# Chain ends and layer outputs of a CIN kernel: from a PSUM bank to SBUF, and a ring of six banks

## The chip, the cores and the metric

One NeuronCore of a Trainium2 chip runs the kernel. The metric is the device time of one launch in microseconds. The engines are TensorE (PE), VectorE (DVE), ScalarE (ACT) and GpSimd (POOL); SyncE (SP) issues DMAs. On-chip data lies in SBUF or in PSUM, where the matmuls of this kernel write. The kernel uses eight PSUM tensors of 512 fp32 columns, called banks below.

## The reference, cut to what matters

512 samples, 48 embedding fields of 32 elements each, gathered from 48 tables. Three "CIN" layers of 128 outputs follow, and a small top network:

```python
def _cin_layer(xi, x0, W, b):                     # xi (n, Fi, 32), x0 (n, 48, 32)
    Wr = W.reshape(Fi, 48, 128)
    out = jnp.einsum('nie,nje,ijo->noe', xi, x0, Wr) + b[None, :, None]
    return jax.nn.relu(out)
xs = [x0]
for W, b in ((W1, b1), (W2, b2), (W3, b3)):
    xs.append(_cin_layer(xs[-1], x0, W, b))
z = jnp.concatenate(xs, axis=1).sum(axis=-1)      # (512, 48 + 3*128)
h = relu([z, dense_ctx] @ W_top1 + b_top1); h = relu(h @ W_top2 + b_top2); y = h @ W_top3
```

## The kernel before

**Tiles.** A tile is 128 samples at one embedding position, so there are 4 x 32 = 128 tiles, and each goes through all three layers. Layer 1 is done through squares of pair sums and is short. For layers 2 and 3 (in the code `layer` 0 and 1) PE computes, for each of 48 fields j, y_j = x W_j of 128x128: twelve "items" a layer, each of four fields, which fill one PSUM bank `y` of 512 columns with three matmuls (hi by whi, hi by wlo, lo by whi; L474). Then out = b + sum over j of x0[:, j] * y_j has to be formed, by two routes. Items marked D in `TAKES` go to DVE, which runs for each field one `scalar_tensor_tensor` acc = y * x0_j + acc (L786; L780 and L782 are the first two of a layer). Two accumulator chains alternate, and the last instruction of each chain writes not `acc` but `chain_end` (two per layer). Items marked A go to ACT, which writes the products y * x0_j to `work` in SBUF (L572); POOL adds them up: a DMA with accumulation (L327) folds two banks of products onto two others, tensor_tensor instructions (L338, L342, L350, L352, L354, L357) sum the rest down to `psum` (an SBUF tile in spite of its name).

**Merging.** DVE's `merge` joins both: msum = chain_end[0] + psum (L795), then outp = chain_end[1] + msum (L800), where `outp` of layers 2 and 3 lies on top of chain_end[0]. From `outp` ACT forms the relu with its row sum (L609, layers 1 and 2), and the high half `hi` (L616); DVE forms the low half `lo` = outp * sc - hi (L832, layers 1 and 2) and adds relu(outp) to the pooled sums (`over_e`, L839, all three layers). SP transposes hi and lo by DMA for PE. `outp` of layer 1 lies in the bank misc[0].

**Order.** All engines run the same software pipeline of `step(v)`: in step v, PE does the twelve items of layer 2 for tile v+1 (n = 0 to 11), the twelve of layer 3 for tile v (n = 12 to 23), with layer 1 of tile v+2 and the pair sums of tile v+3 between them. The order on each engine is written out by hand. DVE's items are n = 1, 3, 5, 7, 9, 11 and 12, 14, 16, 18, 20, 22, 23. In one DVE step the merge instructions stand behind these FMAs: `lo` of layer 2 at n = 5, k = 0, `over_e` of layer 2 at n = 5, k = 1; the two merges of layer 3 at n = 9, k = 0 and 2 (between them `lo` of layer 1, then its `over_e`); `over_e` of layer 3 at n = 11, k = 0; the two merges of layer 2 at n = 20, k = 1 and 3. POOL's order in a step is: last sums of layer 3 (L350 to L357), L327 for layer 2, the scaling of x0 every other step (L368, L373), one gather DMA, L338, L342 and the last sums of layer 2, L327 for layer 3, the low half of the squares (L362, nine times 128 columns), a second gather, L342 of layer 3. The gathers of the next 32 tiles' embeddings run in 24 of the 32 steps of each of the first three blocks of samples, and four steps more copy them out (L304, `spread`); the last block has none.

**Banks.** PSUM holds `RING` = 5 banks `ybank`, two `misc` banks (layer 1 and the pair sums) and the bank `ends`, which holds the four chain ends of layers 2 and 3 and with them their `outp`. PE's item n of a step goes to ybank[n % RING]; `bank_free` makes it wait until DVE or ACT is done with the item that had the bank before (`bank_done`). With 24 items a step and RING = 5 the ring starts anew in every step: items 0 to 3 take the banks of items 20 to 23 of the step before, item 4 that of item 19, the others that of the item five back. At the very end the pooled sums are transposed through ybank[0] to [2] and `ends`.

Of the kernel before, what the change touches and what calls it, by code (L numbers as in the profile page):

```python
# [33 lines left out]
P = 128  # L34
# [11 lines left out]
Z = KT * P  # L46
Q = 4
BANKS = F // Q
RING = 5
HID1, HID2 = 512, 256  # L50


# [15 lines left out]
PAIRS_AT = (12, 14, 17)  # L68
LAST_USER = [max(m for m in range(BANKS) if (BANKS + m) % RING == r) for r in range(RING)]
SCALE = 4  # L70
# [8 lines left out]
def build(nc, ids, tables, ctx_in, select, pairs_of, w_pair, w_pair_t, w2, w3, b_cin, wt1, bt1, wt2, bt2, wt3, out):  # L79
    f32, f16, i32, u32 = mybir.dt.float32, mybir.dt.float16, mybir.dt.int32, mybir.dt.uint32  # L80
    ALU, ACT, AX = mybir.AluOpType, mybir.ActivationFunctionType, mybir.AxisListType

    with ExitStack() as stack:
        def sb(name, shape, dt=f32):
            return stack.enter_context(nc.sbuf_tensor(name, shape, dt))

        def ps(name, shape, dt=f32):
            return stack.enter_context(nc.psum_tensor(name, shape, dt))

        def sem(name):  # L90
            return stack.enter_context(nc.semaphore(name))

        def wait(eng, s, value):

            if not (isinstance(value, int) and value <= 0):
                eng.wait_ge(s, value)  # L96
# [30 lines left out]
        eye32 = sb("eye32", [P, P])  # L127
# [20 lines left out]
        pooled = sb("pooled", [P, NB + 1, 3, P])  # L148
        low = sb("low", [P, NB, F + CTX])
        hT = sb("hT", [P, 4, B])  # L150
# [12 lines left out]

        ybank = [ps(f"y{n}", [P, Q * P]) for n in range(RING)]
        misc = [ps(f"m{n}", [P, Q * P]) for n in range(2)]
        ends = ps("ends", [P, Q * P])

        chain_end = [[ends[:, (2 * l + c) * P:(2 * l + c + 1) * P] for c in range(CHAINS)] for l in range(2)]

# [37 lines left out]
        s_tt, s_tts, s_low, s_h1p, s_h1, s_h2p, s_h2, s_yp, s_ys, s_out = (  # L207
            sem(n) for n in ("hT_in_psum", "hT_saved", "low_ready", "h1_in_psum", "h1_ready", "h2_in_psum",
                             "h2_ready", "y_in_psum", "y_saved", "y_stored"))

        def bank_done(eng, layer, tile, n):

            if n in A_BANKS[layer]:
                wait(eng, s_prod[layer], tile * PRODS[layer] + Q * (A_BANKS[layer].index(n) + 1))
            else:
                wait(eng, s_fma[layer], tile * FMAS[layer] + Q * (D_BANKS[layer].index(n) + 1))
# [12 lines left out]
        def active(tile):  # L229

            return not isinstance(tile, int) or 0 <= tile < TILES
# [186 lines left out]
        def _(pe):  # L418
# [4 lines left out]
            for k in range(KT):  # L423
                ins = nc.tensor.matmul(misc[0][0:F, 0:P], member[:, k, :], w1s[:, k, :], start=k == 0, stop=k == KT - 1)
# [3 lines left out]
            for g in range(2):  # L428
                ins = nc.tensor.transpose(misc[0][0:1, g * P:(g + 1) * P], wmax[:, 8 + g:9 + g], eye32[:])
# [38 lines left out]
            def y_item(layer, t, m, parity):  # L468
                if m == 0:
                    wait(pe, s_xt[layer], (t + 1) * 32)  # L470
                dst = ybank[(layer * BANKS + m) % RING]
                cols = slice(m * Q * P, (m + 1) * Q * P)
# [4 lines left out]
            def bank_free(v, n):  # L477


                for back, first in ((0, n - RING), (1, 2 * BANKS - 1)):  # L480
                    for i in range(first, -1, -1):
                        layer, tile = i // BANKS, v + 1 - i // BANKS - back
                        if i % RING == n % RING and active(tile):
                            return bank_done(pe, layer, tile, i % BANKS)
# [17 lines left out]
            last = TILES - 1  # L502
            pe.wait_ge(s_top, 8 * 16)
            for l in (0, 1):
                pe.wait_ge(s_pool[l], TILES + 1)
                bank_done(pe, 1, last, LAST_USER[l])
                for b in range(NB):
                    ins = nc.tensor.transpose(ybank[l][:, b * P:(b + 1) * P], pooled[:, b, l, :], eye32[:])
# [3 lines left out]
            for b in range(NB):  # L512
                ins = nc.tensor.transpose(ybank[2][0:F + CTX, b * P:(b + 1) * P], low[:, b, :], eye32[:])
# [6 lines left out]
            for i, c in enumerate(CHUNKS):  # L520
                if i == 2:
                    pe.wait_ge(s_pool[2], TILES + 1)
                    for b in range(NB):
                        ins = nc.tensor.transpose(ends[:, b * P:(b + 1) * P], pooled[:, b, 2, :], eye32[:])
                    ins.then_inc(s_tt, 1)
                pe.wait_ge(s_tts, i + 1)
                k = F + CTX if c == 0 else P
                for m in range(HID1 // P):
                    ins = nc.tensor.matmul(h1bank[m][:], wt1_sb[0:k, c, m * P:(m + 1) * P], hT[0:k, c, :],
                                           start=i == 0, stop=c == 3)  # L530
                    if c == 3:
                        ins.then_inc(s_h1p, 1)
            for c in range(HID1 // P):
                pe.wait_ge(s_h1, c + 1)
                for m in range(HID2 // P):
                    ins = nc.tensor.matmul(ybank[m][:], wt2_sb[:, c, m * P:(m + 1) * P], h1[:, c, :],
                                           start=c == 0, stop=c == HID1 // P - 1)
                    if c == HID1 // P - 1:
                        ins.then_inc(s_h2p, 1)
            for c in range(HID2 // P):  # L540
                pe.wait_ge(s_h2, c + 1)
                ins = nc.tensor.matmul(ybank[2][0:1, :], wt3_sb[:, c:c + 1], h2[:, c, :],
                                       start=c == 0, stop=c == HID2 // P - 1)
# [4 lines left out]
        def _(act):  # L548

            act.wait_ge(s_wchain, 16)  # L550
            for l in range(2):
                nc.scalar.activation(whi[l][:], raw[l], ACT.Copy, scale=winv[:, 0:1]).then_inc(s_split, 1)
                for n in range(BANKS):
                    i = l * BANKS + n
                    if i >= RING:
                        act.wait_ge(s_setup, W1_SETUP + i - RING + 1)
# [94 lines left out]
            for i, c in enumerate(CHUNKS):  # L651
                k = F + CTX if c == 0 else P
                act.wait_ge(s_tt, i + 1)
                nc.scalar.activation(hT[0:k, c, :], (ybank[2], ybank[0], ybank[1], ends)[c][0:k, :], ACT.Copy).then_inc(s_tts, 1)
            act.wait_ge(s_top, 8 * 16)
            h1bank = [misc[0], misc[1], ybank[3], ybank[4]]
            for m in range(HID1 // P):
# [297 lines left out]
```

## Time and profile before

| | us |
|---|---|
| median of 3 runs (2443.72 to 2446.77) | 2445.55 |
| the profiled execution | 2444.75 |
| its span in the trace | 2442.9 |
| work before the first item of layer 2 (loads, scales, weights split) | 85.2 |
| last item of layer 3 starts | 2415.0 |

| engine | busy us | share of the span |
|---|---|---|
| PE | 2325.3 | 95% |
| DVE | 2278.7 | 93% |
| ACT | 2117.9 | 87% |
| POOL | 1953.0 | 80% |

Busy time is the union of the instructions' spans. An instruction's duration in the trace is longer than the distance at which the next one follows, so a duration is not what an instruction costs: cost is the distance from one start to the next on the same engine. Three numbers with slashes are the least, median and greatest duration of a group in ns.

### The profile page before, as it was taken

What the parts mean: (1) busy time and instruction counts of PE and PEld (TensorE: products, weight loads), DVE (VectorE), ACT (ScalarE), POOL (GpSimd) and SP (SyncE); (2) the same over time, 40 slices, a digit from 0 to 9 for tenths busy, and PEclk for the clock granted to TensorE, in tenths of its full rate; (3) what the DMA queues carried; (4) which work ended last, traced back from release to release, by engine and by line L of the source; (5) the groups of instructions that cost most, each with busy time, mean ns of one, the idle gap of its engine ahead of it and who ended that gap; (6) DMA issues with size and microseconds to landing.
All of it is one profiled execution on the core that took longest, in us unless ns stands there. A gap on an engine that the chain in (4) does not pass through costs nothing.

```text
span 2442.9 us, 68954 instructions
## 1 busy us (share of the span) xinstructions
PE 2325.3 (95%) x14174; PEld 1178.2 (48%) x14174; DVE 2278.7 (93%) x9404; ACT 2117.9 (87%) x7910; POOL 1953.0 (80%) x2134
## 2 busy tenths in 40 slices
PE   1699999999999999999999999999999999999998
PEld 0354454454554554444455445445445555555543
DVE  6499999999999999999999999999999999999995
ACT  4589889889898898888898888988889989999984
POOL 7488888887778888888778888888777777777773
PEclk6799999999999999999999999999999999999999
DMA  5133333333333333333333333333333333333331
GB/s 170 30 68 72 69 66 70 70 69 64 69 70 66 69 72 70 63 72 70 61 70 70 70 64 71 72 65 68 70 62 70 67 69 70 69 70 69 69 64 35
DMA packets 150318, 168.63 MB, mean 69 GB/s; under 512 B 111956, under 2 KB 115671, under 8 KB 150264
## 3 DMA queue, kind: packets, MB, share of 16 engines
q0 software_dynamic: 43008, 137.39, 30.4%
q1 hardware_dynamic: 107256, 30.73, 5.7%
q14 instruction: 46, 0.38, 0.1%
q8 instruction: 8, 0.13, 0.0%
HBM read 12.82 MB, written 0.00 MB: 5 GB/s over the span
## 4 chain that ended last, share of the span: by engine, by line
PE 42%; POOL 16%; issue 13%; ACT 10%; DVE 9%; DMA 8%; DVEq 1%; ACTq 0%; POOLq 0%; SPq 0%
PE y L474 35%; DMA work<-work 8%; ACT work L572 6%; DVE acc L786 5%; PE m L464 5%; POOL part L350 4%; POOL emb L295 3%; POOL part L354 2%; POOL part L352 2%; ACT work L602 1%; POOL psum L357 1%; POOL rest L342 1%; PE m L446 1%; POOL work L327 1%; DVEq L96 1%
## 5 line engine op out<-in xcount | busy, mean ns | idle before, releaser
L474 PE MATMUL y<-whi,xT 128*128 128x512 f16 x6144 | 2006.9, 379 | 38.8 <-DVE acc L786 24.3
L572 ACT ACTIVATE work<-y,xc 128x128 f32<-128x128 f32 x5632 | 1604.9, 417 | 182.7 <-PE y L474 172.1
L786 DVE SCALAR_TENSOR_TENSOR acc<-y,xc,acc 128x128 f32<-128x128 f32 x5632 | 1654.5, 343 | 32.8 <-PE y L474 24.1
L474 PE MATMUL y<-wlo,xT 128*128 128x512 f16 x3072 | 1164.8, 379 | 0.0
L474 PEld LDWEIGHTS y<-whi,xT 128*128 128x128 f16 x6144 | 599.0, 97 | 692.3 <-issue 77.9
L474 PEld LDWEIGHTS y<-wlo,xT 128*128 128x128 f16 x3072 | 300.8, 98 | 227.8 <-issue 0.6
L350 POOL TENSOR_TENSOR part<-work 128x512 f32<-128x512 f32 x256 | 325.4, 1271 | 90.8 <-DMA work<-work 66.5
L362 POOL TENSOR_TENSOR zl<-work,zh 128x1152 f16<-128x1152 f32 x128 | 345.0, 2695 | 8.1 <-ACT work L602 8.1
L327 POOL DMA_DIRECT2D work<-work x256 | 229.2, 895 | 128.4 <-ACT work L572 127.0
L295 POOL DMA_INDIRECT emb<-tbl,ids_sb x192 | 202.5, 1055 | 45.0 <-issue 43.9
L600 ACT ACTIVATE zh<-m 128x512 f16<-128x512 f32 (+1 forms) x384 | 212.2, 553 | 3.1 <-PE m L446 3.1
L602 ACT ACTIVATE work<-m 128x512 f32<-128x512 f32 (+1 forms) x384 | 214.9, 560 | 0.0
L338 POOL TENSOR_TENSOR part<-work 128x512 f32<-128x512 f32 x128 | 164.5, 1285 | 54.2 <-ACT work L572 54.2
L352 POOL TENSOR_TENSOR part<-part 128x256 f32<-128x256 f32 x256 | 186.0, 727 | 20.1
L354 POOL TENSOR_TENSOR part<-part,rest 128x256 f32<-128x256 f32 x256 | 186.0, 727 | 20.1
L446 PE MATMUL m<-x0T,sel 96*128 96x128 f16 x1280 | 136.1, 220 | 51.5 <-DMA x0T<-x0hl 43.7
L446 PEld LDWEIGHTS m<-x0T,sel 96*128 96x128 f16 x1280 | 100.9, 98 | 149.3 <-issue 43.8
L786 DVE SCALAR_TENSOR_TENSOR ends<-y,xc,acc 128x128 f32<-128x128 f32 x512 | 164.0, 350 | 0.0
L357 POOL TENSOR_TENSOR psum<-part 128x128 f32<-128x128 f32 x256 | 116.4, 455 | 20.1
L464 PE MATMUL m<-w1l,zh 128*128 128x128 f16 x1152 | 127.1, 220 | 0.0
L795 DVE TENSOR_TENSOR msum<-ends,psum 128x128 f32<-128x128 f32 x256 | 73.2, 286 | 55.6 <-POOL psum L357 54.8
L464 PEld LDWEIGHTS m<-w1l,zh 128*128 128x128 f16 x1152 | 91.5, 98 | 59.9
(104 smaller groups left out, 2101.3 us busy)
## 6 DMA issues: line engine op xcount, KB each, us to landing
work<-work POOLq DMA_DIRECT2D x256, 512.0 KB, 4.7
xT<-hi SPq DMA_TRANSPOSE x256, 2.7
xT<-lo SPq DMA_TRANSPOSE x256, 2.4
emb<-tbl,ids_sb POOLq DMA_INDIRECT x192, 2.6
xx<-w SPq DMA_DIRECT2D x4, 768.0 KB, 8.7
work<-w SPq DMA_DIRECT2D x4, 768.0 KB, 14.6
x0T<-x0hl SPq DMA_TRANSPOSE x128, 2.2
wt_sb<-W_top SPq DMA_DIRECT2D x1, 768.0 KB, 13.8
```

The lines of the kernel that those rows point to most:

```text
L295: pool.indirect_dma_start(emb[:, b, f, :], None, tables[f], bass.IndirectOffsetOnAxis(ap=ids_sb[:, b, f:f + 1], axis=0)).then_inc(landed o ...
L327: pool.dma_start(p[:, 0:ADDED, :], p[:, ADDED:2 * ADDED, :], accum_op=ALU.add).then_inc(s_dma[layer], 16)
L350: pool.tensor_tensor(a[:], p[:, 0, :], p[:, 1, :], ALU.add).then_inc(s, 1)
L352: pool.tensor_tensor(a[:, 0:2 * P], a[:, 0:2 * P], a[:, 2 * P:4 * P], ALU.add).then_inc(s, 1)
L354: pool.tensor_tensor(a[:, 0:2 * P], a[:, 0:2 * P], rest[layer][:], ALU.add).then_inc(s, 1)
L362: pool.tensor_tensor(zl[:], zT[:, 0:KF, :], zh[:], ALU.subtract).then_inc(s_zl, 1)
L446: ins = nc.tensor.matmul(misc[PAIR_BANK[g]][:, (k % 4) * P:(k % 4 + 1) * P], sel[:, k * P:(k + 1) * P], x0T[0:2 * F, :], start=True, stop= ...
L464: ins = nc.tensor.matmul(misc[0][:, 0:P], z, w, start=i == 0, stop=i == L1_PASSES - 1)
L474: ins = nc.tensor.matmul(dst[:], xT[layer][:, parity, a, :], w[layer][:, cols], start=i == 0, stop=i == 2)
L572: nc.scalar.activation(prods[layer][:, a, k * P:(k + 1) * P], bank[:, k * P:(k + 1) * P], ACT.Copy, scale=xc[layer][:, parity, j:j + 1]).t ...
L602: nc.scalar.activation(zT[:, 4 * g:4 * g + n, :].rearrange("p t c -> p (t c)"), misc[PAIR_BANK[g]][:, 0:n * P], ACT.Square, scale=SQUARE). ...
L786: ins = nc.vector.scalar_tensor_tensor(dst, y, col, mine, ALU.mult, ALU.add)
```

## The change

`ends` moves from PSUM to SBUF, same shape and type, and with it chain_end and outp of layers 2 and 3. The bank that it leaves becomes a sixth `ybank`. With RING = 6 every item n takes the bank of the item six back, across steps too, since 24 is a multiple of six. The last transpose of the pooled sums goes to ybank[5] in place of `ends`. The setup's ring over the weight banks is six deep as well.

```diff
-RING = 5
+RING = 6
...
-        ends = ps("ends", [P, Q * P])
+        ends = sb("ends", [P, Q * P])
...
                     pe.wait_ge(s_pool[2], TILES + 1)
+                    bank_done(pe, 1, last, LAST_USER[5])
                     for b in range(NB):
-                        ins = nc.tensor.transpose(ends[:, b * P:(b + 1) * P], pooled[:, b, 2, :], eye32[:])
+                        ins = nc.tensor.transpose(ybank[5][:, b * P:(b + 1) * P], pooled[:, b, 2, :], eye32[:])
...
-                nc.scalar.activation(hT[0:k, c, :], (ybank[2], ybank[0], ybank[1], ends)[c][0:k, :], ACT.Copy).then_inc(s_tts, 1)
+                nc.scalar.activation(hT[0:k, c, :], (ybank[2], ybank[0], ybank[1], ybank[5])[c][0:k, :], ACT.Copy).then_inc(s_tts, 1)
```

## Rows read from the trace of the kernel before

**Rows 1.** Page: busy time of each engine and share of the span.

```profile
PE 2325.3 (95%) x14174; PEld 1178.2 (48%) x14174; DVE 2278.7 (93%) x9404; ACT 2117.9 (87%) x7910; POOL 1953.0 (80%) x2134
```

**Rows 2.** Waits, whole span: engine and line, waited for; us, times, longest.

```profile
DVE msum L795 <- POOL psum L357: 54.8, 97, 5.7
...
PE y L474 <- DVE acc L786: 24.3, 47, 1.2
```

**Rows 3.** Line 765, once a step: whole run, gather stretch, stretch without gathers.

```profile
L765 DVE TENSOR_TENSOR zst<-m,zst x128: 282/283/284, 76.1 to 2363.7; 24x128 f16<-24x128 f32 x128
...
L765 DVE TENSOR_TENSOR zst<-m,zst x16: 282/283/284, 738.4 to 1010.8; 24x128 f16<-24x128 f32 x16
...
L765 DVE TENSOR_TENSOR zst<-m,zst x23: 282/284/284, 1866.0 to 2256.2; 24x128 f16<-24x128 f32 x23
```

**Rows 4.** Timelines (start, duration), a step boundary while gathers run: DVE, PE, POOL.

```profile
1045.70 0.29 DVE L795 TENSOR_TENSOR msum<-ends,psum 128x128 f32<-128x128 f32 x1 [0.68 <-POOL psum L357]
...
1046.42 0.29 DVE L800 TENSOR_TENSOR ends<-ends,msum 128x128 f32<-128x128 f32 x1
...
1046.64 0.39 PE L474 MATMUL y<-whi,xT 128*128 128x512 f16 x1 [0.41 <-DVE acc L786]
...
1046.47 2.72 POOL L362 TENSOR_TENSOR zl<-work,zh 128x1152 f16<-128x1152 f32 x1
```

**Rows 5.** By source line: DVE instructions with one operand in PSUM.

```profile
L786 DVE SCALAR_TENSOR_TENSOR ends<-y,xc,acc x512: 336/351/360, 97.5 to 2416.8; 128x128 f32<-128x128 f32 x171
...
L832 DVE SCALAR_TENSOR_TENSOR lo<-ends,sc,hi x128: 331/341/346, 107.8 to 2403.2; 128x128 f16<-128x128 f32 x128
```

**Rows 6.** By source line: DVE instructions with all operands in SBUF.

```profile
L749 DVE TENSOR_SCALAR mx<-mx x64: 157/377/1836, 68.2 to 2312.3; 128x2 f32<-128x2 f32 x64
...
L753 DVE TENSOR_SCALAR mp<-mx x64: 151/570/1223, 68.4 to 2313.0; 128x2 uint32<-128x2 uint32 x64
...
L815 DVE TENSOR_SCALAR tot<-tot x256: 132/144/154, 80.5 to 2400.5; 128x1 f32<-128x1 f32 x128
```

**Rows 7.** Timelines, a stretched L753 on DVE and POOL beside it.

```profile
1198.26 1.22 DVE L753 TENSOR_SCALAR mp<-mx 128x2 uint32<-128x2 uint32 x1
...
1198.19 1.26 POOL L350 TENSOR_TENSOR part<-work 128x512 f32<-128x512 f32 x1
```

**Rows 8.** Timelines, one step without gathers: DVE first, then ACT, then POOL.

```profile
2114.52 0.28 DVE L765 TENSOR_TENSOR zst<-m,zst 24x128 f16<-24x128 f32 x1
...
2119.91 0.35 DVE L786 SCALAR_TENSOR_TENSOR acc<-y,xc,acc 128x128 f32<-128x128 f32 x1 [0.32 <-PE y L474]
2120.18 0.34 DVE L832 SCALAR_TENSOR_TENSOR lo<-ends,sc,hi 128x128 f16<-128x128 f32 x1
...
2124.95 0.28 DVE L839 SCALAR_TENSOR_TENSOR pooled<-ends,pooled 128x128 f32 x1
...
2125.93 0.34 DVE L780 SCALAR_TENSOR_TENSOR acc<-y,xc,bcin 128x128 f32<-128x128 f32 x1
...
2130.72 0.28 DVE L795 TENSOR_TENSOR msum<-ends,psum 128x128 f32<-128x128 f32 x1
...
2131.43 0.29 DVE L800 TENSOR_TENSOR ends<-ends,msum 128x128 f32<-128x128 f32 x1
...
2132.01 0.28 DVE L765 TENSOR_TENSOR zst<-m,zst 24x128 f16<-24x128 f32 x1
...
2130.09 2.26 ACT L572 ACTIVATE work<-y,xc 128x128 f32<-128x128 f32 x8
...
2120.03 0.73 POOL L352 TENSOR_TENSOR part<-part 128x256 f32<-128x256 f32 x1
...
2124.83 1.26 POOL L338 TENSOR_TENSOR part<-work 128x512 f32<-128x512 f32 x1 [1.92 <-ACT work L572]
...
2131.62 0.88 POOL L327 DMA_DIRECT2D work<-work  x1 [1.18 <-ACT work L572]
2132.21 2.69 POOL L362 TENSOR_TENSOR zl<-work,zh 128x1152 f16<-128x1152 f32 x1
```

## The prediction

> **What bounds the kernel now.** I read the page first, then the waits, then one line's starts to get the step's length, then timelines of single steps.
>
> The page shows PE busy for 95% of the span and DVE for 93% [rows 1]. So both matter, and the waits say how they are tied. PE stands 24.3 us for DVE's FMAs in 47 waits, and DVE stands 54.8 us in 97 waits for POOL's `psum` at its first merge [rows 2].
>
> Line 765 runs once a step, so its first and last start give the step: (2363.7 - 76.1)/127 = 18.01 us over the run, (1010.8 - 738.4)/15 = 18.16 us while gathers run, (2256.2 - 1866.0)/22 = 17.74 us without them [rows 3]. In the last stretch PE hardly waits. The pace of PE alone is thus about 17.7 us, and the rest of the mean step, 18.01 - 17.74 = 0.27 us, or 127 x 0.27 = 34 us in all, is what waits cost.
>
> The timeline of a step boundary shows how [rows 4]: DVE waits 0.68 us for `psum` at L795, in the middle of item 20, and PE's item 0 of the next step, which takes item 20's bank with only three items between, starts 0.41 us late. POOL is late because of its gathers.
>
> How much time has DVE left? The step from 2114.52 to 2132.01 is 17.49 us, with about 0.4 us of waiting for PE at item 5 (0.32 us of it named) [rows 8] and some 0.1 us at other items, so DVE's own work is about 17.0 us in a step without x0 scaling. The step before it, with the scaling, is longer by some 0.4 us. I take 17.2 us as DVE's own work per step: slack of 0.5 us against PE's 17.7.
>
> **The change part by part.** The sum is made for the profiled execution, 2444.75 us (its span is 2442.9); the median of the runs is 2445.55, so the two are taken as one.
>
> *The sixth bank.* Item 0 will take the bank of item 18, item 2 that of item 20. That gives PE two items more, at least 1.3 us (three matmuls 0.22 us apart each), before DVE's late item 20 can stop it. The waits seen at item 0 are shorter than that (24.3 us in 47, the longest 1.2 [rows 2]). Alone, this edit is worth up to 34 us. It does nothing for DVE's own 17.2 us.
>
> *FMAs that write `ends`.* L786 with `ends` as output takes 351 ns in the median [rows 5], the one at 2119.91 with `acc` in SBUF 0.35 us [rows 8]. They still read y from PSUM. Taken at 0; bounds +-10 ns for four a step, +-5 us. ACT's relu and `hi` read SBUF in place of PSUM; ACT has 13% idle time, taken at 0, bounds +-0.1 us a step hidden behind that idle time. The changed last transpose and the setup ring: 0, bounds +-2 us once.
>
> *Seven DVE instructions a tile lose their only PSUM operand.* These are L795 and L800 for layers 2 and 3 (four), L839 for layers 2 and 3 (two), and L832 for layer 2 (one). After the change both tensor inputs lie in SBUF. The trace has no such instruction while POOL computes, so its price must be bounded.
>
> From below: nothing. DVE instructions with one operand in PSUM don't feel POOL: L832 on `ends` takes 331 to 346 ns, though POOL's L352 runs beside it [rows 5, 8], and L815, all in SBUF but with one element per partition, takes 132 to 154 ns [rows 6].
>
> From above: L749 and L753, all in SBUF, two elements per partition. They need 157 and 151 ns undisturbed and up to 1836 and 1223 ns [rows 6]. The timeline shows why: L753 starts at 1198.26 and ends at 1199.48, and POOL's L350 runs from 1198.19 to 1199.45 [rows 7]. DVE stood until POOL's instruction was over, and for nearly all of it. A wait is then what POOL's instruction has left, less 0.1 us.
>
> I take the upper end: the seven are all-SBUF instructions with tensor operands, and L749 and L753 are the nearest rows. I can't tell from the rows that what stops them is a matter of SBUF inputs and not of their form.
>
> The Trainium skill ("SBUF — State Buffer", Who interferes with whom) says that a VectorE instruction with two SBUF inputs contends with a GpSimd instruction that reads SBUF, and that whichever comes second blocks until the first is done. By that rule all seven wait, and with at most one SBUF input they would not; the trace agrees on the second half (rows 5) and can't show the first.
>
> What would each wait be? I lay DVE's step over POOL's [rows 8]:
> - `lo` (L832) at 2120.18 meets L352, which ends at 2120.76: 0.58 left, a wait of 0.5; over several steps I take 0.35.
> - L839 of layer 2 comes half a microsecond later, by then in the next POOL instruction (0.73 us long): 0.25.
> - Both merges of layer 3 at n = 9 fall where POOL waits for ACT: 0.05 together.
> - L839 of layer 3 at 2124.95 has just met L338 (2124.83, 1.26 us): 1.0 in this step, nothing in steps where it comes earlier: 0.35.
> - The first merge of layer 2 (2130.72) comes just after `psum`, when POOL issues a DMA: 0.
> - The second merge of layer 2 (2131.43) comes 0.78 us before L362 (2132.21), and in the gather stretch 0.05 us before it [rows 8, 4]. L362 runs 2.7 us.
>
> The first five lines sum to 1.0 us, so DVE reaches item 20 about 1 us later against POOL. Then its second merge is inside L362, with 2.2 us or so left: a wait of 2.1 us.
>
> Does POOL move back too, so that the two stay apart? POOL's L362 follows L327, which waits for ACT's item 19. When DVE is late, PE's items 18 and 19 hang on the banks of items 12 and 13. After DVE's item 12 is done, PE needs 1.3 us for two items, ACT 1.1 us for the four products of item 19 (eight take 2.26), L362 follows L327 by 0.6 us [rows 8]: 3.0 us, and I allow 1 us more for what ACT has before item 19 and for the signals between engines. L362 starts 3.0 to 4.0 us after DVE's item 12. DVE's second merge starts 2131.43 - 2125.93 - 1.1 = 4.4 us after it (the item's four FMAs take the 1.1) [rows 8]. So L362 comes first, and the wait stays in every step.
>
> The step becomes 17.2 + 1.0 + 2.1 = 20.3 us, say 20.2. DVE is then the bound; PE's gain from the sixth bank is gone, since a ring only evens out, and the waits for `psum` go too, as DVE comes later. Time: 2445 + 127 x (20.2 - 18.01) = 2445 + 278 = 2723. I say 2720 us.
>
> **The rivals.**
> - *A, the waits come without L362.* DVE's second merge still just escapes L362, as it does now; only the short waits are paid: 17.2 + 1.0 = 18.2, plus up to 0.6 us of `psum` waits in gather steps, 18.4 on average. 2445 + 127 x 0.4 = 2495. For it: the phases of today, and that DVE waits for `psum` anyway in gather steps. Against it: those phases leave 0.05 to 0.8 us of room, and the short waits are 1 us.
> - *B, the change does what it says (the other side).* All-SBUF inputs cost nothing; what stretches L749 and L753 is their form. Then PE runs at 17.7 in gather steps too: 2445 - 34 = 2411. The point from which it decides is DVE's slack: while the seven waits sum to less than 0.5 us a step, PE sets the pace and the kernel is faster; above that DVE does. For it: L815 isn't touched [rows 6]. Against: the two nearest rows are.
> - *C, no change.* The waits cost about as much as the bank gives (some 0.8 us a step), or POOL paces the gather steps and the bank is hidden: 2445.
> - *D, more than one long hit.* Both merges of layer 2 fall into L362, or those of layer 3 into L338 and L342: one microsecond more, 21.2: 2445 + 127 x 3.2 = 2850.
>
> **How the numbers follow.** Forecast (2600 to 2800): 0.45. A and what lies between (2460 to 2600): 0.32. D: 0.11. B: 0.08. C: 0.04. A measurement of this kernel tells about 0.2%, 5 us, from no change. Slower: 0.45 + 0.32 + 0.11 = 0.88; same 0.04; faster 0.08. The range leaves out B and C (0.12), the least of A and the far end of D: 2485 to 2840.
>
> **What would show it.** Right: L795, L800, L839 on `ends` and L832 on `ends` with a greatest duration of 1 us and more and ends 0.05 to 0.2 us behind the end of a POOL instruction, while L839 and L832 on `m` stay at 280 and 350 ns; DVE's idle for `psum` nearly gone; PE waiting for L786 far longer than 24 us; L800's mean the largest, near 1.3 us, through L362. A: L800 short, and the step 18.3. Wrong: the seven within 20 ns of today. Then the step goes to 17.7 and item 0 waits no more.

## The result and the profile after

The changed kernel takes 2682.28 us (median of 6 runs, 2681.74 to 2682.63), the one before 2445.39 us beside it (6 runs, 2443.72 to 2446.77): ratio 1.0967, 95% interval 1.0954 to 1.0981. It is slower by 237 us. The profiled execution took 2681.77 us, its span is 2680.0. Behind the added line L523 the lines of the changed kernel are one higher than before: L787 is the FMA of L786, L796 and L801 the merges of L795 and L800, L833 `lo`, L840 `over_e`, L766 the step's mark.

The page (engine, busy us, share of the span, instructions), which answers to [rows 1]:

```profile
PE 2405.0 (90%) x14174; PEld 1170.1 (44%) x14174; DVE 2555.8 (95%) x9404; ACT 2112.8 (79%) x7910; POOL 1968.1 (73%) x2134
```

DVE has the same 9404 instructions and is busy for 277 us more, which is more than the kernel lost. The lost time is thus not idle time of DVE. It lies inside DVE's instructions. By source line (count: least/median/greatest duration in ns, first and last start), which answers to [rows 3, 5, 6]:

```profile
L766 DVE TENSOR_TENSOR zst<-m,zst x128: 283/283/284, 76.2 to 2600.1; 24x128 f16<-24x128 f32 x128
...
L801 DVE TENSOR_TENSOR ends<-ends,msum x256: 272/281/4225, 106.3 to 2660.5; 128x128 f32<-128x128 f32 x128
...
L840 DVE SCALAR_TENSOR_TENSOR pooled<-ends,pooled x256: 271/287/1290, 111.2 to 2660.8; 128x128 f32 x122, 128x128 f32<-128x128 f32 x6
L840 DVE SCALAR_TENSOR_TENSOR pooled<-m,pooled x128: 274/280/283, 82.0 to 2609.3; 128x128 f32 x122, 128x128 f32<-128x128 f32 x6
...
L833 DVE SCALAR_TENSOR_TENSOR lo<-m,sc,hi x128: 336/351/353, 81.7 to 2608.4; 128x128 f16<-128x128 f32 x128
L833 DVE SCALAR_TENSOR_TENSOR lo<-ends,sc,hi x128: 332/341/1136, 110.7 to 2640.9; 128x128 f16<-128x128 f32 x128
...
L787 DVE SCALAR_TENSOR_TENSOR ends<-y,xc,acc x512: 325/337/345, 98.3 to 2654.3; 128x128 f32<-128x128 f32 x171
```

The medians of these lines have hardly moved; the greatest durations have, and only where both tensor inputs lie in SBUF. On one and the same line, `over_e` reaches 1290 ns with `ends` and 283 with `m`, which is in PSUM; `lo` reaches 1136 and 353. The step is (2600.1 - 76.2)/127 = 19.87 us.

Where they are stretched is seen in the timelines (start, duration) of DVE, one step and the next, while gathers run [rows 4]:

```profile
1102.72 1.27 DVE L840 SCALAR_TENSOR_TENSOR pooled<-ends,pooled 128x128 f32 x1
...
1104.69 0.34 DVE L781 SCALAR_TENSOR_TENSOR acc<-y,xc,bcin 128x128 f32<-128x128 f32 x1
...
1109.34 0.28 DVE L796 TENSOR_TENSOR msum<-ends,psum 128x128 f32<-128x128 f32 x1
1109.54 0.60 DVE L787 SCALAR_TENSOR_TENSOR acc<-y,xc,acc 128x128 f32<-128x128 f32 x2
1110.06 2.82 DVE L801 TENSOR_TENSOR ends<-ends,msum 128x128 f32<-128x128 f32 x1
...
1113.17 0.28 DVE L766 TENSOR_TENSOR zst<-m,zst 24x128 f16<-24x128 f32 x1
...
1124.32 0.28 DVE L840 SCALAR_TENSOR_TENSOR pooled<-ends,pooled 128x128 f32 x1
...
1125.30 0.34 DVE L781 SCALAR_TENSOR_TENSOR acc<-y,xc,bcin 128x128 f32<-128x128 f32 x1
...
1131.20 0.28 DVE L801 TENSOR_TENSOR ends<-ends,msum 128x128 f32<-128x128 f32 x1
...
1131.77 0.28 DVE L766 TENSOR_TENSOR zst<-m,zst 24x128 f16<-24x128 f32 x1
...
1153.30 0.28 DVE L766 TENSOR_TENSOR zst<-m,zst 24x128 f16<-24x128 f32 x1
```

And POOL in the same stretch:

```profile
1102.58 1.26 POOL L338 TENSOR_TENSOR part<-work 128x512 f32<-128x512 f32 x1 [0.42 <-ACT work L573]
...
1110.01 2.72 POOL L362 TENSOR_TENSOR zl<-work,zh 128x1152 f16<-128x1152 f32 x1
...
1124.79 1.27 POOL L338 TENSOR_TENSOR part<-work 128x512 f32<-128x512 f32 x1
...
1131.80 2.71 POOL L362 TENSOR_TENSOR zl<-work,zh 128x1152 f16<-128x1152 f32 x1
```

L801 starts at 1110.06, 0.05 us behind L362, and ends at 1112.88, 0.15 us behind L362's end. L840 ends at 1103.99, again 0.15 us behind L338's end at 1103.84. One step later L840 starts 0.47 us ahead of L338 and L801 0.60 us ahead of L362; both run in 0.28 us. So the steps alternate: 18.60 us (1113.17 to 1131.77) and 21.53 us (1131.77 to 1153.30). The short one is the step in which POOL scales x0, which puts L338 behind L373 and out of the way of L840. (L840 meets L373 there, which has only 96 columns. None of the 63 all-SBUF instructions that met L368 or L373 in the changed kernel was delayed by more than 0.12 us.)

I summed over all steps what each of the seven takes above its undisturbed duration. The second merge of layer 2 has 175 us, 165 of them in the steps without the scaling of x0 (it is held in 59 of these, for 2.8 us on average, so 2.6 us taken over all of them); `over_e` of layer 3 has 64 (1.0 us in every second step); `lo` of layer 2 has 26, its `over_e` 19, the merges otherwise 9. Together that is 293 us, 2.3 us a step. In 229 cases one of the seven took over 0.45 us because of a POOL instruction that reads SBUF. Each of the 229 ends 0.15 to 0.16 us behind the end of a POOL instruction.

Waits, which answer to [rows 2] (engine and line, waited for: us, times, longest):

```profile
PEld y L474 <- DVE acc L787: 194.9, 261, 3.4
...
PE y L474 <- DVE acc L787: 83.8, 166, 3.3
PE m L446 <- DVE pooled L840: 56.1, 98, 2.3
DVE msum L796 <- POOL psum L357: 39.7, 65, 5.5
```

PE now stands for DVE, and DVE for `psum` a little less than before (54.8).

### The profile page after: what moved, and what is told of

It is laid out like the page before. It is cut to its first block, busy times and chain, and to the rows that moved or that the text cites. A ratio compares the mean times of both kernels' runs of the same rounds, so it can differ in the third digit from the quotient of the medians.

```text
span 2680.0 us, 68955 instructions
## 1 busy us (share of the span) xinstructions
PE 2405.0 (90%) x14174; PEld 1170.1 (44%) x14174; DVE 2555.8 (95%) x9404; ACT 2112.8 (79%) x7910; POOL 1968.1 (73%) x2134
## 4 chain that ended last, share of the span: by engine, by line
DVE 35%; issue 28%; PE 25%; POOL 5%; DVEq 4%; ACT 1%; DMA 1%; ACTq 0%; POOLq 0%; SPq 0%
DVE acc L787 22%; PE y L474 21%; DVEq L96 3%; DVE msum L796 2%; POOL emb L295 2%; PE m L464 2%; DVE pooled L840 2%; DVE acc L781 1%; DVE ends L787 1%; DVE mpw L828 1%; DVE tot L816 1%; PE m L446 1%; DVEq L840 1%; ACT work L573 1%; DVE mp L820 1%
## 5 line engine op out<-in xcount | busy, mean ns | idle before, releaser
L474 PE MATMUL y<-whi,xT 128*128 128x512 f16 x6144 | 2027.9, 381 | 125.6 <-DVE acc L787 83.8
L787 DVE SCALAR_TENSOR_TENSOR acc<-y,xc,acc 128x128 f32<-128x128 f32 x5632 | 1642.4, 339 | 7.9 <-PE y L474 3.6
L362 POOL TENSOR_TENSOR zl<-work,zh 128x1152 f16<-128x1152 f32 x128 | 345.0, 2695 | 8.1 <-ACT work L603 8.1
L801 DVE TENSOR_TENSOR ends<-ends,msum 128x128 f32<-128x128 f32 x256 | 247.5, 967 | 0.3
L295 POOL DMA_INDIRECT emb<-tbl,ids_sb x192 | 203.0, 1058 | 44.9 <-issue 43.8
L446 PE MATMUL m<-x0T,sel 96*128 96x128 f16 x1280 | 136.4, 221 | 102.4 <-DVE pooled L840 56.1
L610 ACT ACTIVATE ends<-ends 128x128 f32<-128x128 f32 x128 | 48.2, 377 | 215.1 <-DVE ends L801 215.1
L338 POOL TENSOR_TENSOR part<-work 128x512 f32<-128x512 f32 x128 | 162.1, 1266 | 69.5 <-ACT work L573 69.5
L446 PEld LDWEIGHTS m<-x0T,sel 96*128 96x128 f16 x1280 | 93.9, 98 | 221.9 <-DVE pooled L840 115.8
L787 DVE SCALAR_TENSOR_TENSOR ends<-y,xc,acc 128x128 f32<-128x128 f32 x512 | 160.7, 337 | 0.0
L840 DVE SCALAR_TENSOR_TENSOR pooled<-ends,pooled 128x128 f32 (+1 forms) x256 | 154.5, 603 | 0.1
```

The costliest lines, as they stand in the source:

```text
L295: pool.indirect_dma_start(emb[:, b, f, :], None, tables[f], bass.IndirectOffsetOnAxis(ap=ids_sb[:, b, f:f + 1], axis=0)).then_inc(landed o ...
L362: pool.tensor_tensor(zl[:], zT[:, 0:KF, :], zh[:], ALU.subtract).then_inc(s_zl, 1)
L446: ins = nc.tensor.matmul(misc[PAIR_BANK[g]][:, (k % 4) * P:(k % 4 + 1) * P], sel[:, k * P:(k + 1) * P], x0T[0:2 * F, :], start=True, stop= ...
L474: ins = nc.tensor.matmul(dst[:], xT[layer][:, parity, a, :], w[layer][:, cols], start=i == 0, stop=i == 2)
L787: ins = nc.vector.scalar_tensor_tensor(dst, y, col, mine, ALU.mult, ALU.add)
L801: nc.vector.tensor_tensor(outp[layer + 1], chain_end[layer][1], msum[layer][:], ALU.add).then_inc(s_pre[layer + 1], 1)
```

## The experiments

The first theory: two SBUF inputs make a DVE instruction stand until the POOL instruction that is running is over. Its rivals: the all-SBUF form is slower as such; the loss comes from the sixth bank or the changed ring; the stretched time is off the path. Ratios are to the kernel before, run beside each, with their 95% intervals behind them.

**e1: SBUF alone, ring of five.**

```diff
-RING = 6
+RING = 5
...
-        ybank = [ps(f"y{n}", [P, Q * P]) for n in range(RING)]
+        ybank = [ps(f"y{n}", [P, Q * P]) for n in range(RING + 1)]
```

> One part alone: ends in SBUF as in the changed kernel, but RING = 5 (the last transpose has its own bank). Port theory (a DVE instruction whose tensor inputs both lie in SBUF stands until POOL's running instruction is over): slow like the changed kernel, 2682 us, or more by what the sixth bank softens, 2680 to 2760; L801 with a greatest duration over 2.6 us. Rival (the sixth bank and its new order do the harm): back near 2445 us.

Measured: 2771.07 us, ratio 1.1338 (1.1319 to 1.1357). The sixth bank does no harm. With DVE held up it gives back 2771 - 2682 = 89 us. PE's waits for DVE's FMAs (matmuls and weight loads together) are 519 us here and 303 with six banks: PE gets further ahead before DVE's long stall stops it.

The long hit is here too, but it comes about otherwise. The second merge of layer 2, then L362:

```profile
1133.77 3.28 DVE L800 TENSOR_TENSOR ends<-ends,msum 128x128 f32<-128x128 f32 x1
1134.17 2.72 POOL L362 TENSOR_TENSOR zl<-work,zh 128x1152 f16<-128x1152 f32 x1
```

The merge starts 0.40 us ahead of L362 and is held to its end all the same. In this run all 59 second merges that start 0.25 to 0.43 us ahead of L362 are held, and none of the 61 that start 0.55 us ahead or more. To come first by the start times is not enough.

**e2 and e3: the seven with one SBUF input, rings of six and five.** The seven become `tensor_reduce` over an axis of length one, in the same places and with the same waits. The other summand is left out, so these kernels leave out a part of the computation.

```diff
-                    nc.vector.tensor_tensor(outp[layer + 1], chain_end[layer][1], msum[layer][:],
-                                            ALU.add).then_inc(s_pre[layer + 1], 1)
+                    nc.vector.tensor_reduce(outp[layer + 1], chain_end[layer][1].unsqueeze(2), axis=AX.X,
+                                            op=ALU.max).then_inc(s_pre[layer + 1], 1)
```

> The changed kernel, but the seven DVE instructions a tile read one SBUF tensor each (a tensor_reduce over an axis of size 1 in place of the addition; the other summand is left out, so part of the computation is missing). Outputs and chain ends still lie in SBUF, RING = 6. Port theory by the number of inputs: none of the seven is longer than 0.4 us, the time falls to 2411 us (2400 to 2430), the sixth bank's 34 us below the kernel before. Rival 1 (any all-SBUF instruction waits, as L749 and L753): the durations stay up to 2.7 us and the time near 2680. Rival 2 (writing chain ends or outputs to SBUF costs): in between.

> As the one before (seven instructions with one SBUF input, the other summand left out), but RING = 5: with it, it gives what the sixth bank is worth when DVE is not held up. Port theory: 2445 us (2435 to 2455), so the bank is worth 20 to 40 us. Rival (the bank is worth nothing, POOL paces the steps with gathers): within 5 us of the run with six banks.

Measured: 2428.59 us with six banks (ratio 0.9941, 0.9925 to 0.9958) and 2431.40 with five (0.9947, 0.9930 to 0.9964). With six banks, by source line:

```profile
L801 DVE TENSOR_REDUCE ends<-ends x256: 268/276/287, 103.3 to 2405.8; 128x128 f32<-128x128 f32 x128
...
L834 DVE TENSOR_REDUCE lo<-hi x128: 264/275/278, 107.7 to 2385.8; 128x128 f16<-128x128 f16 x128
...
L844 DVE TENSOR_REDUCE pooled<-ends x256: 264/275/288, 108.1 to 2406.1; 128x128 f32 x122, 128x128 f32<-128x128 f32 x6
```

All data lie in SBUF, POOL's work is untouched, and not one of the 896 instructions takes more than 290 ns, though 237 of them run in the middle of a POOL instruction. Data in SBUF alone cost these instructions nothing. These runs change the operation along with the number of inputs; that it is the second SBUF input is shown by one and the same operation in the changed kernel, `scalar_tensor_tensor`, held with `ends` and not with `m`. The Trainium skill ("SBUF — State Buffer", Who interferes with whom) says just that: a VectorE instruction with two SBUF inputs contends with a GpSimd instruction that reads SBUF, and `tensor_reduce` on trn2 never does; these runs agree.

The pair also prices the bank with DVE undisturbed: 2.8 us by the medians, with four runs each whose ranges touch (2427.08 to 2430.57 and 2429.26 to 2432.05), so hardly more than nothing and not the up to 34 of the prediction. The waits of e3, then of e2:

```profile
DVE msum L795 <- POOL psum L357: 43.3, 67, 5.4
...
PE y L474 <- DVE acc L786: 19.5, 50, 1.2
...
PE m L446 <- DVE pooled L845: 4.6, 9, 2.1
```

```profile
DVE msum L796 <- POOL psum L357: 67.2, 117, 5.7
...
PE m L446 <- DVE pooled L846: 19.9, 40, 2.1
PE y L474 <- DVE acc L787: 2.4, 4, 0.9
```

PE's wait for y goes, 19.5 to 2.4 us; its wait at the pair sums (L446, whose bank DVE has to leave first) grows by 15, and DVE's for `psum` by 24. The waiting moved on to the next things that DVE and POOL are late with. (The one-input forms are also a little shorter, `lo` 275 in place of 341 ns. DVE's busy time in e3 is 13 us below that of before, which fits the 12 us that e3 gains with five banks.)

**e4: L362 cut in three.**

```diff
-                pool.tensor_tensor(zl[:], zT[:, 0:KF, :], zh[:], ALU.subtract).then_inc(s_zl, 1)
+                for c in range(0, KF, 3):
+                    ins = pool.tensor_tensor(zl[:, c:c + 3, :], zT[:, c:c + 3, :], zh[:, c:c + 3, :], ALU.subtract)
+                ins.then_inc(s_zl, 1)
```

> The changed kernel with POOL's L362 (2.7 us) cut into three of three columns each (some 0.95 us); the computation is whole. Port theory: the longest wait of L801 falls from 2.7 to about 1 us, and some 1.6 us every second step are saved: 2682 - 64 x 1.6 = 2580 us (2540 to 2640), though POOL has 0.2 us more a step. Rival (sharing of bandwidth and not a lock for an instruction's length): L801 stays as long, 2680 us.

Measured: 2713.20 us, ratio 1.1102 (1.1083 to 1.1120), slower than the changed kernel. The expectation was wrong: the merge should have waited for one piece. DVE, then POOL:

```profile
1120.06 3.07 DVE L803 TENSOR_TENSOR ends<-ends,msum 128x128 f32<-128x128 f32 x1
...
1119.98 2.99 POOL L363 TENSOR_TENSOR zl<-work,zh 128x384 f16<-128x384 f32 x3
```

The merge stands through all three pieces, as it does in 59 steps. The rival written down beforehand, shared bandwidth in place of a wait for whole instructions, foretold this too. In this trace each piece starts 0.39 us before the one ahead of it ends (1119.98 to 1121.24, 1120.85 to 1122.11, 1121.72 to 1122.97), so the second reading is that DVE gets no turn between POOL instructions that overlap.

**e9: the same pieces, each waiting for the one before.** This tests that reading against shared bandwidth.

```diff
+                for i in range(3):
+                    c = 3 * i
+                    wait(pool, s_zl, t * 3 + i)
+                    pool.tensor_tensor(zl[:, c:c + 3, :], zT[:, c:c + 3, :], zh[:, c:c + 3, :],
+                                       ALU.subtract).then_inc(s_zl, 1)
```

> The changed kernel with L362 cut into three, and each piece waits for the semaphore of the piece before, so POOL pauses between them. Theory T (DVE gets its turn only when POOL's train of instructions pauses: in the split without waits L801's counterpart stood through all three pieces, up to 3.07 us in that timeline): now the wait is one piece, the longest about 1.1 us, some 1.7 us less every second step, 2682 - 64 x 1.7 = 2573 us (2540 to 2620). Rival (the wait depends on where DVE comes against POOL, not on trains; the pieces just shift): 2680 to 2720 as without the waits.

Measured: 2639.80 us (2634.69 to 2640.92), ratio 1.0797 (1.0779 to 1.0815). The same place, POOL and DVE in one timeline:

```profile
1129.38 3.24 POOL L365 TENSOR_TENSOR zl<-work,zh 128x384 f16<-128x384 f32 x3
1129.45 1.34 DVE L805 TENSOR_TENSOR ends<-ends,msum 128x128 f32<-128x128 f32 x1
```

With a wait between the pieces DVE gets in after the first: 1.34 us in place of 3.07. The first piece ends at 1130.63 and the next starts 0.08 us later; the merge ends at 1130.79, 0.16 us behind the first piece, while the other two still run. The same goes for 64 of the 65 second merges that are held here: they are done at the end of one piece, which shared bandwidth does not explain. That merge's extra time falls from 184 to 65 us over the run and the kernel gains 73 us on e4. It doesn't gain the 140 us expected, in part because DVE comes earlier to what follows: the scaling's L758 (L753 before) is now held for 51 us in place of 19.

**e5: L362 as a memset, which reads nothing.** It leaves out the low half of the squares.

```diff
-                pool.tensor_tensor(zl[:], zT[:, 0:KF, :], zh[:], ALU.subtract).then_inc(s_zl, 1)
+                pool.memset(zl[:], 0.0).then_inc(s_zl, 1)
```

> The changed kernel with L362 replaced by a memset of zl (so the low half of the squares is left out): POOL writes the same tile and reads nothing. Port theory with reads only: the second merge of layer 2 no longer stands long (under 0.5 us), the others (L840, L833) do; 2682 - 64 x 2.6 = 2516 us (2480 to 2580), part of it for POOL's shorter instruction. Rival (POOL's writes hold DVE as well): the merge stands for as long as the memset runs.

Measured: 2476.53 us, ratio 1.0128 (1.0107 to 1.0148). POOL, then DVE in the middle of it:

```profile
1089.40 1.44 POOL L362 MEMSET zl<- 128x1152 f16 x1
1089.49 0.28 DVE L801 TENSOR_TENSOR ends<-ends,msum 128x128 f32<-128x128 f32 x1
```

POOL writes and DVE's two-input merge runs beside it in its 0.28 us. All 59 second merges that start inside the memset take 0.27 to 0.29 us. So it is POOL's reads that hold DVE. `over_e` of layer 3 is still held for 64 us by L338. The memset is also another operation than the subtraction and shorter (1.44 for 2.72 us), so the time of this kernel is not the price of L362 alone; the row is.

**e6 and e7: only layer 2's, or only layer 3's ends in SBUF, ring of five.**

```diff
+        ends_sb = sb("ends_sb", [P, Q * P])
+        at = [ends, ends]
+        at[0] = ends_sb              # e7: at[1] = ends_sb
...
-        chain_end = [[ends[:, (2 * l + c) * P:(2 * l + c + 1) * P] for c in range(CHAINS)] for l in range(2)]
+        chain_end = [[at[l][:, (2 * l + c) * P:(2 * l + c + 1) * P] for c in range(CHAINS)] for l in range(2)]
```

> The kernel before (RING = 5), but only layer 2's chain ends and output in SBUF: two merges at n = 20, lo and over_e at n = 5. Port theory: the second merge is up to 0.8 us before L362 without the 1.0 us wait of layer 3's over_e ahead of it, so it hits L362 in part of the steps (13 of 36 odd gather steps lay inside it before); lo and over_e cost 0.3 to 0.6 us. 2500 us (2450 to 2620). Rival (the waits simply add: 176 + 45 us of the changed kernel's): 2660 us.

> The kernel before (RING = 5), but only layer 3's chain ends and output in SBUF: the merges at n = 9 (never met POOL in the changed kernel) and over_e at n = 11, which stood 1.0 us in every second step. Port theory: that wait stays, 64 x 1.0 = 63 us, partly in DVE's slack: 2475 us (2450 to 2510). Together with the run on layer 2 this shows whether the two parts add up to 2771 us (both, RING = 5), or feed each other.

Measured: 2515.24 us (ratio 1.0287, 1.0270 to 1.0304) and 2502.12 us (1.0234, 1.0217 to 1.0251), against 2445.21 beside them. Layer 2 alone:

```profile
L803 DVE TENSOR_TENSOR ends_sb<-ends_sb,msum 128x128 f32<-128x128 f32 x128 | 43.2, 338 | 0.1
...
L835 DVE SCALAR_TENSOR_TENSOR lo<-ends_sb,sc,hi 128x128 f16<-128x128 f32 x128 | 91.4, 714 | 0.0
L842 DVE SCALAR_TENSOR_TENSOR pooled<-ends_sb,pooled 128x128 f32 x122 | 72.3, 592 | 0.0
```

Its second merge takes 338 ns on average (busy us, mean ns stand behind the bar): it misses L362 in all but 2 steps. Its loss is `lo` and `over_e`. Layer 3 alone costs by `over_e`, 861 ns on average where 285 is undisturbed. Apart they cost 70 + 57 = 127 us. Together, in e1, they cost 328. The 200 us between are the long hit (195 us on the second merges in e1). The starts show what brings it in. In the steps without the scaling, layer 2's second merge starts 0.93 us ahead of L362 in e6 (median), but 0.41 us ahead in e7, where layer 3's `over_e` has lost 1.0 us before it, and 0.40 us ahead in e1. In e7 this merge still has an input in PSUM and is not held; in e1 it is all-SBUF, and 0.40 us is too little. With six banks it comes later still, 0.07 us behind L362's start.

**e8, e10, e11, e12: what is to be had without the change.** The kernel before, with POOL's second gather ahead of `add_by_dma(1, t3)` and L362 (e8); with L749 and L753 cut into instructions of one element per partition, as L815 has (e10); with both (e11); and with the merges of layer 2 later besides (e12).

```diff
                     sum_all(0, t2)
+                gather(b, fields[1:2])
                 if active(t3):
...
                     squares_lo(t0)
-                gather(b, fields[1:2])
```

```diff
-                    nc.vector.tensor_scalar(mx0[:, 1, :], mx0[:, 0, :], TINY0, HALF_RANGE, ALU.max, ALU.mult).then_inc(s, 1)
+                    for j in range(2):
+                        ins = nc.vector.tensor_scalar(mx0[:, 1, j:j + 1], mx0[:, 0, j:j + 1], TINY0, HALF_RANGE, ALU.max, ALU.mult)
+                    ins.then_inc(s, 1)
```

```diff
-                        if n == 20 and k % 2 == 1 and active(t2):
-                            merge(0, t2, k // 2)
+                        if n == 20 and k == 3 and active(t2):
+                            merge(0, t2, 0)
+                        if n == 22 and k == 0 and active(t2):
+                            merge(0, t2, 1)
```

> The kernel before (ends in PSUM, RING = 5) with POOL's second gather of a step moved ahead of L327 for layer 3, into the 0.6 us in which POOL waits for ACT's item 19 in gather steps. If psum coming late holds DVE and through item 20's bank PE: gather steps fall from 18.14 towards 17.8 us, up to 25 us, 2420 to 2440. Rival (another wait takes its place, L362 or layer 3's sums late): 2443 to 2455.

> The kernel before with L749 and L753 each cut into two instructions of one element per partition, the form that was never stretched (L815: 154 ns at most). Port theory: their 42 us of waiting go (0.7 us in every second step), at a price of 0.12 us; gain in the steps with gathers and with spreads, where DVE holds PE: 2425 to 2440. Rival (they sit in DVE's slack): 2445.

> Both edits on the kernel before. If the gains add: 2405 to 2430. If DVE's wait for psum was the only binding one: as the better of the two.

> Both edits, and DVE's merge of layer 2 after the last FMA of item 20 (first part) and after item 22's first FMA (second part), so that item 20's bank is free before DVE waits for psum: what the sixth bank was to give, with five. If item 20's bank is what holds PE: 2400 to 2420. Rival (relu, scale and lo of layer 2 come late in turn, or PE then waits for the pair sums' bank as in the run with one input and six banks): same as without it, or some us more.

| kernel | us | ratio to before (2443.35), 95% |
|---|---|---|
| e8 | 2424.49 | 0.9924 (0.9910 to 0.9938) |
| e10 | 2421.92 | 0.9915 (0.9901 to 0.9929) |
| e11 | 2407.17 | 0.9853 (0.9837 to 0.9869) |
| e12 | 2404.17 | 0.9842 (0.9828 to 0.9856) |

In e10, by source line, against 1836 ns at the worst [rows 6]:

```profile
L750 DVE TENSOR_SCALAR mx<-mx x128: 143/150/158, 68.1 to 2288.8; 128x1 f32<-128x1 f32 x128
```

The 128 instructions of 150 ns are never held, where one of 157 was held for up to 1.7 us. DVE is busy for 29 us less, and the kernel gains 21 of them. In e12, the waits that cost before [rows 2] are much smaller:

```profile
DVE msum L799 <- POOL psum L357: 14.1, 8, 5.4
...
PE y L474 <- DVE acc L790: 2.3, 4, 1.0
```

e12 beats both kernels, by 39 us the one before. The later merges are worth 3 us of it (the fastest run of e11 took 2406.61, the slowest of e12 2405.40).

## Why the prediction was right, and where its sizes were off

The forecast was slower, 2720 us; 2682.28 came. The mechanism is the one it named, and neither B nor C holds. Step by step:

- *What holds L749 and L753 holds all-SBUF instructions.* It was the choice on which all hung, between nothing and POOL's rest. Its outcome was right, but its reason was not, and that was luck. The seven are held because both tensor inputs lie in SBUF; L749 and L753 have one SBUF input and are held nevertheless, and with one input the seven are not (e2). The kinds of holding differ. L749 and L753 end 0.02 to 0.05 us behind POOL's end, the seven 0.15. And in 33 cases in the kernel before it was a gather (L295, a DMA issue) that held L749 or L753, while in the changed kernel 70 of the seven's instructions start inside a gather with 0.2 us or more of it left, and none takes more than 0.29 us. First the kernel before, then the changed one:

```profile
177.54 1.07 POOL L295 DMA_INDIRECT emb<-tbl,ids_sb  x1 [0.17 <-issue]
177.89 0.77 DVE L749 TENSOR_SCALAR mx<-mx 128x2 f32<-128x2 f32 x1
```

```profile
1101.09 1.08 POOL L295 DMA_INDIRECT emb<-tbl,ids_sb  x1 [0.30 <-issue]
1101.80 0.28 DVE L801 TENSOR_TENSOR ends<-ends,msum 128x128 f32<-128x128 f32 x1
```
- *The wait is POOL's rest less 0.1 us.* Right where POOL pauses behind the instruction. L840 at 1102.72 had 1.12 us of L338 left and took 1.27 - 0.28 = 0.99 more; L801 had 2.67 left and took 2.54 more. In 27 of the 229 cases it was the rest of a train of overlapping POOL instructions (last section).
- *The short waits, 1.0 us a step.* 0.9 measured (118 us in all), but otherwise spread: `over_e` of layer 3 took 0.50 a step where 0.35 stood, `lo` of layer 2 0.20 for 0.35, its `over_e` 0.15 for 0.25.
- *The second merge of layer 2 meets L362 in every step, 2.1 us.* This is the mis-sized term. It meets it in every second step, for 2.6 us on average: 175/127 = 1.4 us a step. The argument was that POOL can't fall back with DVE, as L362 starts 3.0 to 4.0 us after DVE's item 12. Item 12 starts at 1104.69 and is done 1.1 us later; L362 comes 4.2 us after that, the merge 4.3. A step later, item 12 starts at 1125.30; L362 comes 5.4 us after its end, the merge 4.8. There PE shows no wait for DVE between item 12 and L362, so L362 isn't tied to DVE's item 12, and the allowance of 1 us was too small in both steps. The forecast laid one step over all; it should have laid both, with and without the scaling of x0.
- *The waits for `psum` go.* They stayed, 39.7 of 54.8 us: in the short steps DVE is as early as before. With them and what else DVE waits for, the sum is 17.2 + 0.9 + 1.4 + 0.4 = 19.9 us, where 0.4 is the rest to the measured 19.87; the prediction had 20.2. That the time came within 38 us is in part luck: 0.7 us a step too much for the long hit and 0.4 us too little for the waits stand against each other.
- *The sixth bank, up to 34 us alone.* Wrong in size: about 3 us, hardly clear of noise, when DVE isn't held (e2, e3), since DVE and POOL were late for the next thing too, and 89 us when it is (e1), where it was said that the gain is gone. A ring evens out, and here the load was uneven.
- *FMAs that write `ends` and ACT's reads, 0.* The FMAs that write `ends` are 14 ns shorter in the median (337 for 351), where the bounds were 10; over 512 of them that is 7 us at most. ACT's busy time fell by 5 us.
- *Rival A.* Its waits without the long hit are what e6 and e7 show each by itself, 2515 and 2502 us; its 2495 was near for one layer, but both layers together bring L362 in. The room of 0.05 to 0.8 us that it counted on was less than it looked, since a merge that starts 0.25 to 0.43 us ahead is held as well (e1). *Rival D*, a second long hit, wasn't there in the changed kernel but in single steps.

What had to be seen in the profile was seen: the seven stretched up to 1 us and more with ends 0.15 us behind POOL's, `over_e` and `lo` on `m` as before, PE waiting for L787 far longer than 24 us. The mean of the second merges was to be 1.3 us; the line's mean is 967 ns.

## What to carry to other kernels

Before an accumulator leaves PSUM, count the DVE instructions that then have both tensor inputs in SBUF, and lay each over POOL's timeline: what each can lose is what POOL's reading instructions have left, a whole train of them if they overlap. Here an instruction that started up to 0.43 us ahead of POOL's was held too. Look for the loss in durations, greatest against median, as the instruction is shown as busy and not as waiting. Where two engines' phases alternate from step to step, lay every kind of step, and remember that a 1 us wait can be dear by what it pushes the next instruction into: two halves of this change cost 127 us apart and 328 together.

## What the runs showed of the hardware that was not expected

A DVE instruction that is held waits for a whole train of POOL instructions where these overlap. Three pieces of L362 held it for 3.07 us, with waits between them for 1.34 us. The changed kernel has such a train too, where no gather lies behind L362 (DVE, then POOL):

```profile
2340.68 3.43 DVE L801 TENSOR_TENSOR ends<-ends,msum 128x128 f32<-128x128 f32 x1
...
2340.59 2.69 POOL L362 TENSOR_TENSOR zl<-work,zh 128x1152 f16<-128x1152 f32 x1
2342.92 1.04 POOL L342 TENSOR_TENSOR rest<-work 128x256 f32<-128x256 f32 x1
```

L362 ends at 2343.28, yet L801 ends at 2344.11, 0.15 us behind L342's end at 2343.96. L342 shows a start 0.36 us before L362's end. The traces tell when DVE gets no turn: in the 27 trains of the changed kernel each POOL instruction starts 0.32 to 0.39 us before the one ahead ends, while in 163 other cases the next one starts a mere 0.08 us after it (L338 ends at 1103.84, L342 starts at 1103.92), and DVE gets in every time. The overlap comes where POOL has no wait for its own result in between, so which of the two decides stays open. The Trainium skill ("SBUF — State Buffer", Who interferes with whom) has the holder keep the shared ports for the whole instruction; these measurements agree for a single POOL instruction and go further for a train, and they decide.

Cutting an instruction can free it: one DVE instruction of two elements per partition was held up to 1.7 us, two of one element never. Why a form with a single SBUF input is held at all, by gathers too, no run here shows.
